# Third attention over the context: another order of four heads' work on every engine, turned groups in other banks

## The chip, the cores and the metric

The kernel runs on one core of one Trainium2 chip. The metric is the device time of one execution in microseconds. The kernel before took 2265.95 us (median of three runs, 2257.9 to 2266.71).

## The reference, cut to what matters

A perceiver of four layers works on 8 sequences of 64 rows with 256 features. In layers 0, 2 and 3 the rows attend to a context of 1601 rows with 128 features. The change touches the last of these, in layer 3, which computes for every batch and each of 16 heads of 16 features:

```
q = x @ Wq.T            k, v = ctx @ Wkv.T
p = softmax(q @ k.T * 16 ** -0.5)       # 64 x 1601 per head
o = (p @ v) @ Wo.T
```

The kernel keeps `p @ ctx` per head and multiplies with the value weights later, and it divides by the softmax's sums later too. Everything is float32: a product that needs the precision is made of three passes over a high and a low part (high x high, high x low, low x high).

## The kernel before, in words

The function `paired_attention` (L1126) holds the whole stage. A *unit* `v` is a pair of heads of one batch: 2 x 64 = 128 query rows, so there are 64 units, 8 per batch. Two units, that is four heads, are a *couple*: 32 couples, 4 per batch (`at` = 0 to 3). A *step* is two batches; the first step, the loop over the middle ones and the last are written by `loop_batches`. Per unit:

- TensorE makes the scores (L1285) in four products with 290, 512, 512 and 288 columns into PSUM banks 0 to 3. The first two are the first half, the last two the second.
- VectorE takes the maximum of each half (L1478, L1480) and joins the two (`ntop`, L1483).
- ScalarE takes the exponent of each half (`exponents`, L1420) into `normed` or `rooms`.
- TensorE turns the 13 chunks of 128 keys in four groups of 4, 4, 4 and 1 (`turn`, L1312) into banks 4, 5 and 7 (`turned_bank`, L1151).
- ScalarE copies each group rounded to `pTh` (`keep`, L1431), and VectorE subtracts it from the same bank into `pTl` (`low`, L1491). Only then is the bank free.
- Per couple TensorE multiplies the context's rows with both units' turned groups (`values`, L1344; its three passes are L616 to L618) in 39 products with 256 columns into bank 6, and VectorE stores the sum (`store`, L1501).

Beside this the keys of the *next* batch are projected, two tiles of 400 or 402 columns per couple (`key_tile`, L1291, three passes each), into bank 7. ScalarE copies a tile out (`keep_key`, L1410) into `key_rows`, POOL splits it (`split_key`, L1240 and L1243), and SyncE moves it in DMAs of 32 rows into `stacked`, the operand of the scores. Such a move (`move(b, at)`, L1184, with `move_half`, L2563) is 12 DMAs. For `at` = 0 and 2 it waits in SyncE's queue until the second scores of couples 1 and 3 are made, since those were the last to read what it overwrites; the move for `at` + 1 follows directly behind it. The other way round, `keep_key` for the first tile of a couple waits until the move that last read that half of `key_rows` has landed (semaphores `moved0`, `moved1`, L1405 to L1408). For couples 0 and 2 that is the move which the couple just before set off.

Every engine works through its own queue in the order written in its `body`. The order of TensorE for one couple before the change is: turn group 0 of the unit before, scores of unit `u`, turn 1, turn 2, values 0, turn 3, values 1, key tile 0, scores of `u + 1`, turn 0 and 1 of `u`, key tile 1, values 2, turn 2, values 3, turn 3. All semaphores count, so the number that an instruction waits for follows from the order.

Of the kernel before, what the change touches and what calls it, by code (L numbers as in the profile page):

```python
# [109 lines left out]
def perceiver_kernel(nc, dram, packs, out):  # L110
    with ExitStack() as stack:
# [1014 lines left out]
        def paired_attention(q, scale, keys, sums):  # L1126
# [8 lines left out]
            with ExitStack() as own, signals(nc, *names) as \  # L1135
# [15 lines left out]
                turned_bank = (4, 5, 7, 4), (5, 7, 4, 5)  # L1151
# [19 lines left out]
                with nc.Block() as block:  # L1171
# [98 lines left out]
                    def _(pe):  # L1270
                        def scores(u, step, first):
                            i = u // PER
                            v = step * UNITS + u
                            if first and i == 0:
                                pe.wait_ge(keys.first_moved[u], 48)
                            elif u % 4 == 0:
                                for sem in moved:
                                    pe.wait_ge(sem, MOVES * (2 * (2 * step + i) - 1 + (u % PER) // 4))
                            if u % 2 == 0:
                                pe.wait_ge(staged, step * COUPLES + u // 2 + 1)  # L1280
                            k, at = (u // 2) % 2, (u % 2) * P
                            for n in range(4):
                                if n in (0, 2) and not (first and u == 0):
                                    pe.wait_ge(probs_ready if n else probs_half, v)
                                last = pe.matmul(flat[:, score_cols[n]], qs[:, k, at:at + P],  # L1285
                                                 keys.stacked[:, u % PER, score_cols[n]], start=True, stop=True)
                                if n == 1:
                                    last.then_inc(scores_half, 1)
                            last.then_inc(scores_ready, 1)

                        def key_tile(u, step, j, final):  # L1291

                            i, at = u // PER, (u // 2) % 4
                            for chunk, tile, n in key_tiles(i, at, final):
                                if n == j:
                                    if at == 0 and j == 0:
                                        pe.wait_ge(low_ready, 2 * (2 * step + i) + 1)
                                    if j == 1:
                                        pe.wait_ge(key_kept, 8 * (2 * step + i) + 2 * at + 1)
                                    project_keys(pe, keys, chunk, tile, 7).then_inc(key_ready, 1)  # L1300

                        def key_bank_free(u, step, final):

                            i, at = u // PER, (u // 2) % 4
                            if key_tiles(i, at, final):
                                pe.wait_ge(key_kept, 8 * (2 * step + i) + 2 * at + 2)
# [9 lines left out]
                        def turn_first(g, v, early=False):  # L1316

                            if g == 0 and not early:
                                pe.wait_ge(low_kept, 4 * v - 1)
                            if g == 1 and not early:  # L1320
                                pe.wait_ge(low_kept, 4 * v)
                            if g == 3:
                                pe.wait_ge(low_kept, 4 * v + 1)
                            turn(g, v, 0)

                        def turn_second(g, v):

                            pe.wait_ge(low_kept, 4 * v + (-2, -1, 0, 1)[g])
                            turn(g, v, 1)

                        def values(g, c, i, early=False, new_batch=None):
# [7 lines left out]
                            pe.wait_ge(low_kept, 4 * (2 * c + 1) + g + 1)  # L1339
# [8 lines left out]
                        def body(step, first, final=False):  # L1348
                            for u in range(0, UNITS, 2):
# [6 lines left out]
                                if first and u == 0:  # L1356
                                    scores(u, step, first)
                                    scores(u + 1, step, first)
                                    for g in range(4):
                                        turn_first(g, v, True)  # L1360
                                    pe.wait_ge(low_kept, 3)
                                    key_tile(u, step, 0, final)
                                    key_tile(u, step, 1, final)
                                    continue
                                pe.wait_ge(probs_half, v)
                                turn_second(0, v - 1)
                                scores(u, step, first)
                                if first and u == 2:
                                    key_bank_free(0, step, final)
                                turn_second(1, v - 1)  # L1370
                                turn_second(2, v - 1)
                                values(0, c - 1, i, first and u == 2, new_batch)
                                turn_second(3, v - 1)
                                values(1, c - 1, i)
                                if key_tiles(u // PER, (u // 2) % 4, final):
                                    pe.wait_ge(low_kept, 4 * v - 2)
                                key_tile(u, step, 0, final)
                                scores(u + 1, step, first)
# [12 lines left out]
                        pe.wait_ge(probs_ready, last + 1)  # L1391
                        for g in range(4):
                            turn_second(g, last)
                        values(0, c, 1)
                        values(1, c, 1)
                        values(2, c, 1)
                        values(3, c, 1)

                    @block.scalar
                    def _(act):  # L1400
                        def keep_key(step, first_step, i, at, tile, j):
# [8 lines left out]
                            nc.scalar.activation(key_rows[:, cols], ps[:, 7, 0:cols.stop - cols.start], ACT.Copy)\  # L1410
# [14 lines left out]
                        def keep(g, v, slot, c=None):  # L1425

                            act.wait_ge(turned_ready, 4 * v + g + 1)
# [8 lines left out]
                        def body(step, first, final=False):  # L1436
                            for u in range(0, UNITS, 2):
# [32 lines left out]
                        for g in range(4):  # L1470
                            keep(g, last, 1)

                    @block.vector
                    def _(dve):
                        def maximum(v, slot):

                            dve.wait_ge(scores_half, v + 1)
                            dve.tensor_reduce(top[:, slot, 0:1], flat[:, half_cols[0]], AX.X, ALU.max).then_inc(top_step, 1)  # L1478
                            dve.wait_ge(scores_ready, v + 1)
# [6 lines left out]
                        def low(g, v, slot):  # L1486

                            dve.wait_ge(high_kept, 4 * v + g + 1)
# [37 lines left out]
                        for g in range(4):  # L1526
# [1806 lines left out]
```

## Time and profile before

| | us |
|---|---|
| median of three runs | 2265.95 |
| the profiled execution's own time | 2265.01 |
| its span, first to last instruction | 2263.2 |
| TensorE busy in the span | 2018.8 (89%) |
| VectorE busy | 1392.2 (62%) |
| ScalarE busy | 1141.2 (50%) |
| POOL busy | 595.6 (26%) |
| mean granted TensorE clock | 0.945 of full speed |

The stage that is changed runs from about 1700 to 2078 us of the span. In it the engines' rows show a pattern that repeats every couple, so one couple, read closely, tells most of the stage. Busy time of TensorE counts overlapping pieces: the distance between the starts of two matmuls, not the duration of one, tells what a matmul costs its queue.

### The profile page before, as it was taken

The page shows a single profiled execution, that of the slowest core. Times are in us where ns is not written, and L with a number is a line of the kernel's source. Part 1 is how long each engine was busy: PE and PEld are TensorE (multiplying, and loading weights), DVE is VectorE, ACT ScalarE, POOL GpSimd, SP SyncE. Part 2 cuts the span into 40 slices and gives each one's busy share as a digit, 9 for nine tenths or more (in the row PEclk, how much of TensorE's full clock was granted, in tenths as well). Part 3 has the DMA queues.
Part 4 walks back from the last instruction along what each step waited for, and adds up shares of the span by engine and source line. Part 5 has one row for each costly group of instructions (what it writes and reads, how often), then busy time and mean ns, then how long its engine had stood idle before and what let it go on. Part 6 is the DMA issues. An engine that isn't in the chain of part 4 may idle for free. (4 is left out here: it accounts for less than half of the span.)

```text
span 2263.2 us, 42827 instructions
## 1 busy us (share of the span) xinstructions
PE 2018.8 (89%) x14978; PEld 1739.0 (77%) x14978; DVE 1392.2 (62%) x2718; ACT 1141.2 (50%) x2324; POOL 595.6 (26%) x536
## 2 busy tenths in 40 slices
PE   5877999999887998589899999988888998998898
PEld 2766999999566885278699999966767888887677
DVE  8455777777355443831577777745456777776466
ACT  3235666666423432321566666633446676665254
POOL 2323212221012330200322222102325555440034
PEclk9798999999996998689999999999998999999899
DMA  5252101000041213431110110002226555551022
GB/s 217 58 233 103 42 31 46 30 30 0 36 149 58 79 54 138 191 133 64 59 46 31 36 39 30 0 0 84 80 71 164 152 138 139 139 132 42 19 79 76
DMA packets 49603, 183.66 MB, mean 81 GB/s; under 512 B 9392, under 2 KB 14896, under 8 KB 46128
## 3 DMA queue, kind: packets, MB, share of 16 engines
q1 hardware_dynamic: 49456, 181.75, 25.0%
q8 instruction: 86, 1.41, 0.3%
q14 instruction: 61, 0.50, 0.1%
HBM read 125.72 MB, written 13.90 MB: 62 GB/s over the span
## 5 line engine op out<-in xcount | busy, mean ns | idle before, releaser
L616 PE MATMUL ps<-pTh,ch 128*128 128x256 f32 (+1 forms) x1248 | 382.3, 306 | 26.2 <-DVE pTl L1491 25.0
L1026 ACT ACTIVATE pTh<-ps 128x512 fp32r<-128x512 f32 (+1 forms) x512 | 235.8, 519 | 258.0 <-PE ps L926 257.7
L617 PE MATMUL ps<-pTl,ch 128*128 128x256 f32 (+1 forms) x1248 | 350.2, 281 | 0.0
L618 PE MATMUL ps<-pTh,cl 128*128 128x256 f32 (+1 forms) x1248 | 349.9, 280 | 0.0
L1084 DVE TENSOR_TENSOR pTl<-ps,pTh 128x512 fp32r<-128x512 f32 (+1 forms) x512 | 277.3, 583 | 83.8 <-ACT pTh L1026 83.2
L616 PEld LDWEIGHTS ps<-pTh,ch 128*128 128x128 f32 (+1 forms) x1248 | 236.1, 189 | 43.0 <-DVE pTl L1491 32.4
L617 PEld LDWEIGHTS ps<-pTl,ch 128*128 128x128 f32 (+1 forms) x1248 | 236.9, 190 | 0.0
L618 PEld LDWEIGHTS ps<-pTh,cl 128*128 128x128 f32 (+1 forms) x1248 | 235.9, 189 | 0.0
L616 PE MATMUL ps<-cTh,qh 128*128 128x512 f32 (+2 forms) x512 | 184.8, 361 | 16.7 <-POOL ql L880 11.9
L618 PE MATMUL ps<-cTh,ql 128*128 128x512 f32 (+2 forms) x512 | 179.9, 351 | 0.0
L617 PE MATMUL ps<-cTl,qh 128*128 128x512 f32 (+2 forms) x512 | 179.5, 351 | 0.0
L1071 DVE TENSOR_REDUCE top<-ps 128x1 f32<-128x802 f32 x128 | 126.3, 987 | 75.2 <-PE ps L618 75.2
L1491 DVE TENSOR_TENSOR pTl<-ps,pTh 128x512 fp32r<-128x512 f32 (+1 forms) x256 | 138.8, 582 | 47.8 <-ACT pTh L1431 47.1
L1431 ACT ACTIVATE pTh<-ps 128x512 fp32r<-128x512 f32 (+1 forms) x256 | 117.7, 514 | 56.1 <-PE ps L1312 56.0
L1073 DVE TENSOR_REDUCE top<-ps 128x1 f32<-128x799 f32 x128 | 125.9, 983 | 10.4 <-PE ps L618 3.8
L1015 ACT ACTIVATE normed<-ps,ntop 128x802 f32<-128x802 f32 (+1 forms) x128 | 117.8, 926 | 20.4 <-DVE ntop L1076 19.1
L926 PE MATMUL ps<-ident,probs 128*128 128x128 f32 (+1 forms) x832 | 122.0, 273 | 2.8 <-ACT probs L1015 1.7
L926 PE MATMUL ps<-ident,normed 128*128 128x128 f32 (+1 forms) x832 | 123.5, 275 | 0.4 <-DVE pTl L1084 0.4
L616 PEld LDWEIGHTS ps<-cTh,qh 128*128 128x128 f32 x512 | 97.9, 191 | 30.6 <-POOL ql L880 13.6
L616 PE MATMUL ps<-xh,wgh 128*128 128x512 f32 (+1 forms) x280 | 113.3, 405 | 5.4 <-DVE gated L1942 4.3
L1015 ACT ACTIVATE probs<-ps,ntop 128x802 f32<-128x802 f32 (+1 forms) x128 | 117.9, 937 | 0.0
L617 PE MATMUL ps<-xl,wgh 128*128 128x512 f32 (+1 forms) x280 | 112.6, 402 | 0.0
(406 smaller groups left out, 4613.2 us busy)
## 6 DMA issues: line engine op xcount, KB each, us to landing
stacked<-weights SPq DMA_DIRECT2D x168, 100.2 KB, 2.2
stacked<-weights SPq DMA_DIRECT2D x168, 100.0 KB, 2.2
w<-l1f_w_in SPq DMA_DIRECT2D x16, 1024.0 KB, 8.2
wg<-l0f_guide_in SPq DMA_DIRECT2D x10, 704.0 KB, 5.2
z<-ctx_in SPq DMA_DIRECT2D x8, 832.0 KB, 12.8
z<-z SPq DMA_DIRECT2D x8, 832.0 KB, 10.0
keys<-ctx_in SPq DMA_DIRECT2D x8, 832.0 KB, 10.7
zT<-zT SPq DMA_DIRECT2D x8, 801.0 KB, 9.1
```

The costliest lines, as they stand in the source:

```text
L616: pe.matmul(out, high, moving_high, start=start, stop=False)
L617: pe.matmul(out, high, moving_low, start=False, stop=False)
L618: return pe.matmul(out, low, moving_high, start=False, stop=stop)
L926: last = pe.transpose(ps[0:w, turned_bank[slot][g], k * P:(k + 1) * P], probs[slot][:, chunk * P:chunk * P + w], ident[:])
L1015: nc.scalar.activation(probs[slot][:, cols], flat[:, cols], ACT.Exp, bias=ntop[:, slot:slot + 1], scale=scale, accum_out=sums[:, bass.ds(2 ...
L1026: nc.scalar.activation(pTh[0:w, PARTS[g][0]:PARTS[g][0] + n, slot, :], ps[0:w, turned_bank[slot][g], 0:n * P].rearrange("p (k r) -> p k r" ...
L1071: dve.tensor_reduce(top[:, slot, 0:1], flat[:, half_cols[0]], AX.X, ALU.max).then_inc(top_step, 1)
L1073: dve.tensor_reduce(top[:, slot, 1:2], flat[:, half_cols[1]], AX.X, ALU.max)\
L1084: dve.tensor_tensor(pTl[0:w, at, slot, :], ps[0:w, turned_bank[slot][g], 0:n * P].rearrange("p (k r) -> p k r", r=P), pTh[0:w, at, slot, : ...
L1431: nc.scalar.activation(pTh[0:w, PARTS[g][0]:PARTS[g][0] + n, slot, :], ps[0:w, turned_bank[slot][g], 0:n * P].rearrange("p (k r) -> p k r" ...
L1491: dve.tensor_tensor(pTl[0:w, at, slot, :], ps[0:w, turned_bank[slot][g], 0:n * P].rearrange("p (k r) -> p k r", r=P), pTh[0:w, at, slot, : ...
```

## The change: what it does

- The scores' halves become separate steps (`first_scores`, `second_scores`), and so do the maxima on VectorE.
- TensorE's order for a couple is now: first scores of `u`, turn group 0 of the unit before, key tile 0, key tile 1, second scores of `u`, turn 1, turn 3, turn 2, values 0, values 1, first and second scores of `u + 1`, turn 1, 0, 2 of `u`, values 2, values 3, turn 3.
- Groups of the even unit go to banks 7, 4, 5, 4, those of the odd unit to 7, 4, 7, 5; the key tiles go to banks 4 and 5 instead of 7.
- ScalarE's order: keep 0, both key tiles, keep 1, keep 3, first exponent, keep 2, second exponent, keep 1, keep 0, first exponent of `u + 1`, keep 2, keep 3, second exponent of `u + 1`.
- VectorE's order: first maximum, low 0, second maximum, low 1, 3, 2, both maxima of `u + 1`, low 1, low 0, store, low 3, low 2.
- The waits' numbers follow the new orders. POOL's and SyncE's programs, the number of instructions and their shapes stay as they are.

```diff
-                turned_bank = (4, 5, 7, 4), (5, 7, 4, 5)
+                turned_bank = (7, 4, 5, 4), (7, 4, 7, 5)
+                turn_place, low_place = ((2, 1, 3, 4), (1, 2, 4, 3)), ((2, 1, 4, 3), (1, 2, 4, 3))
+                key_bank = 4, 5
...
                         def key_tile(u, step, j, final):
...
-                                    if j == 1:
-                                        pe.wait_ge(key_kept, 8 * (2 * step + i) + 2 * at + 1)
-                                    project_keys(pe, keys, chunk, tile, 7).then_inc(key_ready, 1)
+                                project_keys(pe, keys, tiles[j][0], tiles[j][1], key_bank[j]).then_inc(key_ready, 1)
...
-                                pe.wait_ge(probs_half, v)
-                                turn_second(0, v - 1)
-                                scores(u, step, first)
-                                turn_second(1, v - 1)
-                                turn_second(2, v - 1)
-                                values(0, c - 1, i, first and u == 2, new_batch)
-                                turn_second(3, v - 1)
-                                values(1, c - 1, i)
-                                if key_tiles(u // PER, (u // 2) % 4, final):
-                                    pe.wait_ge(low_kept, 4 * v - 2)
-                                key_tile(u, step, 0, final)
-                                scores(u + 1, step, first)
-                                turn_first(0, v)
-                                turn_first(1, v)
-                                key_tile(u, step, 1, final)
-                                values(2, c - 1, i)
-                                key_bank_free(u, step, final)
-                                turn_first(2, v)
-                                values(3, c - 1, i)
-                                turn_first(3, v)
+                                first_scores(u, step, first)
+                                pe.wait_ge(low_kept, 4 * v - 6)
+                                turn(0, v - 1, 1)
+                                pe.wait_ge(low_kept, 4 * v - 5)
+                                key_tile(u, step, 0, final)
+                                pe.wait_ge(low_kept, 4 * v - 4)
+                                key_tile(u, step, 1, final)
+                                second_scores(u, step, first)
+                                key_bank_free(u, step, 0, final)
+                                turn(1, v - 1, 1)
+                                key_bank_free(u, step, 1, final)
+                                turn(3, v - 1, 1)
+                                pe.wait_ge(low_kept, 4 * v - 3)
+                                turn(2, v - 1, 1)
                                 values(0, c - 1, i, first and u == 2, new_batch)
                                 values(1, c - 1, i)
+                                first_scores(u + 1, step, first)
+                                second_scores(u + 1, step, first)
+                                turn(1, v, 0)
+                                pe.wait_ge(low_kept, 4 * v)
+                                turn(0, v, 0)
+                                turn(2, v, 0)
                                 values(2, c - 1, i)
                                 values(3, c - 1, i)
+                                pe.wait_ge(low_kept, 4 * v + 1)
+                                turn(3, v, 0)
...
                                 if before:
                                     keep(0, v - 1, 1)
+                                    for chunk, tile, j in tiles:
+                                        keep_key(step, first, i, at, tile, j)
                                     keep(1, v - 1, 1)
+                                    keep(3, v - 1, 1)
+                                exponents(v, 0, first and u < 2, 0)
+                                if before:
                                     keep(2, v - 1, 1)
-                                exponents(v, 0, first and u < 2, 0)
                                 exponents(v, 0, first and u < 2, 1)
-                                if before:
-                                    keep(3, v - 1, 1)
-                                    for chunk, tile, j in tiles[0:1]:
-                                        keep_key(step, first, i, at, tile, j)
+                                keep(1, v, 0, c if before else None)
                                 keep(0, v, 0, c if before else None)
-                                keep(1, v, 0, c if before else None)
-                                if before:
-                                    for chunk, tile, j in tiles[1:]:
-                                        keep_key(step, first, i, at, tile, j)
                                 exponents(v + 1, 1, first and u < 2, 0)
-                                exponents(v + 1, 1, first and u < 2, 1)
                                 keep(2, v, 0, c if before else None)
                                 keep(3, v, 0, c if before else None)
+                                exponents(v + 1, 1, first and u < 2, 1)
...
+                                first_maximum(v, 0)
                                 if before:
                                     low(0, v - 1, 1)
-                                maximum(v, 0)
+                                second_maximum(v, 0)
                                 if before:
                                     low(1, v - 1, 1)
+                                    low(3, v - 1, 1)
                                     low(2, v - 1, 1)
-                                    low(3, v - 1, 1)
-                                maximum(v + 1, 1)
+                                first_maximum(v + 1, 1)
+                                second_maximum(v + 1, 1)
+                                low(1, v, 0)
                                 low(0, v, 0)
-                                low(1, v, 0)
                                 if before:
                                     store(c - 1, 2 * step + (u - 2) // PER, ((u - 2) // 2) % 4)
+                                low(3, v, 0)
                                 low(2, v, 0)
-                                low(3, v, 0)
```

## Rows read from the trace of the kernel before

**Rows 1.** Busy time of each engine by stretch (stretch, its length, engines in turn).

```profile
core 0: us, PE busy (x) PEld busy (x) DVE busy (x) ACT busy (x) POOL busy (x), PEclk, DMA share, GB/s
1750.00:1800.00 50.00, 45.64 (x344) 42.55 (x343) 38.28 (x66) 34.88 (x77) 28.59 (x31) 1.00 0.58 146
...
1950.00:2000.00 50.00, 45.31 (x340) 42.22 (x339) 37.35 (x65) 34.64 (x78) 24.72 (x28) 1.00 0.55 141
```

**Rows 2.** Waits from 1720 to 2070 us: who for whom, total, times, longest.

```profile
ACT pTh L1431 <- PE ps L1312: 51.2, 61, 2.3
...
PEld ps L616 <- DVE pTl L1491: 32.4, 30, 2.2
PE ps L616 <- DVE pTl L1491: 25.0, 30, 2.0
```

**Rows 3.** Timeline, start of a couple at `at` = 2 (start, us, engine, line).

```profile
1867.14 0.27 PE L1312 MATMUL ps<-ident,rooms 128*65 128x128 f32 x1
...
1867.46 1.28 DVE L1491 TENSOR_TENSOR pTl<-ps,pTh 128x512 fp32r<-128x512 f32 x2
...
1868.20 0.38 PE L616 MATMUL ps<-pTh,ch 128*128 128x256 f32 x1 [0.80 <-DVE pTl L1491]
...
1868.54 0.28 PE L618 MATMUL ps<-pTh,cl 128*128 128x256 f32 x1
1868.66 0.28 PE L616 MATMUL ps<-pTh,ch 128*128 128x256 f32 x1
...
1870.11 0.34 PE L618 MATMUL ps<-cTh,wkl 128*128 128x402 f32 x1
1870.29 0.90 PE L1285 MATMUL ps<-stacked,qs 96*128 96x290 f32 x4
...
1870.58 0.51 ACT L1410 ACTIVATE weights<-ps 128x402 f32<-128x402 f32 x1 [0.81 <-PE ps L618]
...
1871.03 1.04 PE L1312 MATMUL ps<-ident,normed 128*128 128x128 f32 x8
```

**Rows 4.** Timeline of TensorE's weight loads at eight turns and what follows them.

```profile
1859.33 0.93 PEld L1312 LDWEIGHTS ps<-ident,normed 128*128 128x128 f32 x8
...
1860.22 0.19 PEld L616 LDWEIGHTS ps<-cTh,wkh 128*128 128x128 f32 x1
```

**Rows 5.** Timeline of VectorE, the last couples, which project no keys.

```profile
2040.50 0.98 DVE L1478 TENSOR_REDUCE top<-ps 128x1 f32<-128x802 f32 x1
...
2051.41 0.98 DVE L1478 TENSOR_REDUCE top<-ps 128x1 f32<-128x802 f32 x1
```

**Rows 6.** Timeline of SyncE's queue: starts of pairs of moves, 24 DMAs each.

```profile
1836.53 15.72 SPq L2569 DMA_DIRECT2D stacked<-weights  x24
...
1859.65 16.36 SPq L2569 DMA_DIRECT2D stacked<-weights  x24
...
1882.79 15.21 SPq L2569 DMA_DIRECT2D stacked<-weights  x24
```

**Rows 7.** Timeline: the scores ahead of that second start; ScalarE's first tile at `at` = 0.

```profile
1858.72 0.90 PE L1285 MATMUL ps<-stacked,qs 96*128 96x290 f32 x4
...
1859.46 1.04 PE L1312 MATMUL ps<-ident,normed 128*128 128x128 f32 x8
...
1847.45 0.51 ACT L1410 ACTIVATE weights<-ps 128x402 f32<-128x402 f32 x1 [0.80 <-PE ps L618]
```

**Rows 8.** Tile `stacked`, DMAs issued around 1844.0 us: the first move's last two.

```profile
L2569 SPq DMA_DIRECT2D stacked<-weights x2: 597/598/599, 1843.4 to 1844.0; - x2
...
DMA to landing us min/median/max: 2.2/2.2/2.2
```

**Rows 9.** Waits from 1583 to 1590 us, in the feed-forward stage.

```profile
PE ps L616 <- DVE gated L1942: 4.3, 1, 4.3
```

**Rows 10.** Busy time and granted clock behind two pauses of TensorE.

```profile
1889.00:1890.96 1.96, 0.00 (x0) 0.00 (x0) 0.74 (x2) 1.37 (x3) 1.96 (x1) 0.96 0.70 163
1890.96:1894.20 3.24, 3.24 (x15) 3.24 (x16) 3.15 (x5) 1.02 (x2) 1.33 (x3) 0.50 0.70 166
...
1589.08:1593.90 4.82, 4.79 (x11) 3.80 (x12) 2.48 (x4) 2.23 (x4) 2.37 (x1) 0.50 0.36 109
```

More of the change, by code:

```diff
@@ L1270, in _, with first_scores @@
                     def _(pe):
-                        def scores(u, step, first):
+                        def first_scores(u, step, first):
                             i = u // PER
@@ L1280, in scores, with second_scores @@
                                 pe.wait_ge(staged, step * COUPLES + u // 2 + 1)
+                            if not (first and u == 0):
+                                pe.wait_ge(probs_half, v)
+                            score_half(u, 0).then_inc(scores_half, 1)
+                        def second_scores(u, step, first):
+                            if not (first and u == 0):
+                                pe.wait_ge(probs_ready, step * UNITS + u)
+                            score_half(u, 1).then_inc(scores_ready, 1)
@@ L1281, in scores, with score_half @@
+                        def score_half(u, half):
                             k, at = (u // 2) % 2, (u % 2) * P
-                            for n in range(4):
-                                if n in (0, 2) and not (first and u == 0):
-                                    pe.wait_ge(probs_ready if n else probs_half, v)
+                            for n in (2 * half, 2 * half + 1):
                                 last = pe.matmul(flat[:, score_cols[n]], qs[:, k, at:at + P],
                                                  keys.stacked[:, u % PER, score_cols[n]], start=True, stop=True)
-                                if n == 1:
-                                    last.then_inc(scores_half, 1)
@@ L1289, in scores @@
-                            last.then_inc(scores_ready, 1)
+                            return last
                         def key_tile(u, step, j, final):
                             i, at = u // PER, (u // 2) % 4
[L1294 to L1297, printed above, removed]
-                                    if j == 1:
-                                        pe.wait_ge(key_kept, 8 * (2 * step + i) + 2 * at + 1)
-                                    project_keys(pe, keys, chunk, tile, 7).then_inc(key_ready, 1)
@@ L1302, in key_bank_free @@
-                        def key_bank_free(u, step, final):
+                            tiles = key_tiles(i, at, final)
+                            if tiles:
+                                if at == 0 and j == 0:
+                                    pe.wait_ge(low_ready, 2 * (2 * step + i) + 1)
+                                project_keys(pe, keys, tiles[j][0], tiles[j][1], key_bank[j]).then_inc(key_ready, 1)
+                        def key_bank_free(u, step, j, final):
                             i, at = u // PER, (u // 2) % 4
@@ L1305, in key_bank_free @@
                             if key_tiles(i, at, final):
-                                pe.wait_ge(key_kept, 8 * (2 * step + i) + 2 * at + 2)
+                                pe.wait_ge(key_kept, 8 * (2 * step + i) + 2 * at + j + 1)
                         def turn(g, v, slot):
@@ L1314, in turn @@
                             last.then_inc(turned_ready, 1)
[L1316 to L1329, printed above, removed]
                         def values(g, c, i, early=False, new_batch=None):
@@ L1338, in values @@
                                 pe.wait_ge(keys.first_rows, 1)
-                            pe.wait_ge(low_kept, 4 * (2 * c + 1) + g + 1)
+                            if g < 3:
+                                pe.wait_ge(low_kept, 4 * (2 * c + 1) + low_place[1][g])
                             for chunk in PARTS[g]:
@@ L1356, in body @@
                                 if first and u == 0:
-                                    scores(u, step, first)
-                                    scores(u + 1, step, first)
-                                    for g in range(4):
-                                        turn_first(g, v, True)
+                                    for n in range(2):
+                                        first_scores(u + n, step, first)
+                                        second_scores(u + n, step, first)
@@ L1361, in body @@
+                                    turn(1, v, 0)
+                                    turn(0, v, 0)
+                                    turn(2, v, 0)
+                                    pe.wait_ge(low_kept, 1)
+                                    turn(3, v, 0)
                                     pe.wait_ge(low_kept, 3)
                                     key_tile(u, step, 0, final)
+                                    pe.wait_ge(low_kept, 4)
                                     key_tile(u, step, 1, final)
@@ L1364, in body @@
                                     continue
-                                pe.wait_ge(probs_half, v)
-                                turn_second(0, v - 1)
-                                scores(u, step, first)
+                                first_scores(u, step, first)
+                                pe.wait_ge(low_kept, 4 * v - 6)
+                                turn(0, v - 1, 1)
                                 if first and u == 2:
-                                    key_bank_free(0, step, final)
@@ L1370, in body @@
-                                turn_second(1, v - 1)
-                                turn_second(2, v - 1)
+                                    pe.wait_ge(key_kept, 2)
+                                pe.wait_ge(low_kept, 4 * v - 5)
[4 more added lines that the diff above has]
+                                key_bank_free(u, step, 0, final)
@@ L1377, in body @@
-                                key_tile(u, step, 0, final)
-                                scores(u + 1, step, first)
-                                turn_first(0, v)
-                                turn_first(1, v)
-                                key_tile(u, step, 1, final)
+                                first_scores(u + 1, step, first)
+                                second_scores(u + 1, step, first)
+                                turn(1, v, 0)
+                                pe.wait_ge(low_kept, 4 * v)
@@ L1382, in body @@
+                                turn(0, v, 0)
+                                turn(2, v, 0)
                                 values(2, c - 1, i)
-                                key_bank_free(u, step, final)
-                                turn_first(2, v)
                                 values(3, c - 1, i)
-                                turn_first(3, v)
+                                pe.wait_ge(low_kept, 4 * v + 1)
+                                turn(3, v, 0)
                         loop_batches(pe, body)
@@ L1391, in _ @@
                         pe.wait_ge(probs_ready, last + 1)
-                        for g in range(4):
[L1393 to L1397, printed above, removed]
+                        pe.wait_ge(low_kept, 4 * last - 2)
+                        turn(0, last, 1)
+                        pe.wait_ge(low_kept, 4 * last)
+                        turn(1, last, 1)
+                        turn(3, last, 1)
+                        pe.wait_ge(low_kept, 4 * last + 1)
+                        turn(2, last, 1)
+                        for g in range(4):
+                            values(g, c, 1)
                     @block.scalar
@@ L1409, in keep_key @@
                             cols = K_COLS[tile]
-                            nc.scalar.activation(key_rows[:, cols], ps[:, 7, 0:cols.stop - cols.start], ACT.Copy)\
+                            nc.scalar.activation(key_rows[:, cols], ps[:, key_bank[j], 0:cols.stop - cols.start], ACT.Copy)\
                                 .then_inc(key_kept, 1)
@@ L1425, in keep @@
                         def keep(g, v, slot, c=None):
-                            act.wait_ge(turned_ready, 4 * v + g + 1)
+                            act.wait_ge(turned_ready, 4 * v + turn_place[slot][g])
                             if c is not None:
@@ L1469, in _ @@
                         last = STEPS * UNITS - 1
-                        for g in range(4):
+                        for g in (0, 1, 3, 2):
                             keep(g, last, 1)
@@ L1474, in _, with first_maximum, second_maximum @@
                     def _(dve):
-                        def maximum(v, slot):
+                        def first_maximum(v, slot):
                             dve.wait_ge(scores_half, v + 1)
                             dve.tensor_reduce(top[:, slot, 0:1], flat[:, half_cols[0]], AX.X, ALU.max).then_inc(top_step, 1)
+                        def second_maximum(v, slot):
                             dve.wait_ge(scores_ready, v + 1)
@@ L1486, in low @@
                         def low(g, v, slot):
-                            dve.wait_ge(high_kept, 4 * v + g + 1)
+                            dve.wait_ge(high_kept, 4 * v + turn_place[slot][g])
                             w, n = keys_in(PARTS[g][-1]), len(PARTS[g])
@@ L1508, in body @@
                                 before = not (first and u == 0)
+                                first_maximum(v, 0)
                                 if before:
                                     low(0, v - 1, 1)
-                                maximum(v, 0)
+                                second_maximum(v, 0)
                                 if before:
                                     low(1, v - 1, 1)
+                                    low(3, v - 1, 1)
                                     low(2, v - 1, 1)
-                                    low(3, v - 1, 1)
-                                maximum(v + 1, 1)
+                                first_maximum(v + 1, 1)
+                                second_maximum(v + 1, 1)
+                                low(1, v, 0)
                                 low(0, v, 0)
-                                low(1, v, 0)
                                 if before:
                                     store(c - 1, 2 * step + (u - 2) // PER, ((u - 2) // 2) % 4)
+                                low(3, v, 0)
                                 low(2, v, 0)
-                                low(3, v, 0)
                         loop_steps(dve, body)
                         last = STEPS * UNITS - 1
-                        for g in range(4):
+                        for g in (0, 1, 3, 2):
                             low(g, last, 1)
```

## The prediction

> **What bounds the kernel now.** The change touches one stage, 1700 to 2078 us, so I read the busy times of that stretch first: TensorE is busy 45.6 of 50 us, VectorE 38, ScalarE 35, and the clock is full [rows 1]. TensorE is the bound, but not quite. The waits say what it lacks: in 30 of the 32 couples its value products wait for `low` on VectorE, 25.0 us in all [rows 2]. The timeline shows the place. TensorE ends turn group 3 at about 1867.3 and starts values 1 only at 1868.20, since `low(1)` stands on VectorE behind both maxima and `ntop`, starts at 1867.46 and takes 0.6 to 0.7 us [rows 3]. So each couple has a hole of 0.8 to 0.9 us, and a second one near 0.5 us at turn 1.
>
> How long is a couple? Pairs of moves start at 1836.53, 1859.65 and 1882.79, one pair per two couples [rows 6]: two couples take 23.1 us. And what is TensorE's own work in a couple? From starts to starts a value product costs 0.12 us (1868.54 to 1868.66), the scores of a unit 0.74 (1870.29 to 1871.03), a key product 0.18 to 0.19 [rows 3], and eight turns 0.89, or 0.112 each [rows 4]. With 39 products, 26 turns, two sets of scores and six key products: 4.68 + 2.91 + 1.49 + 1.11 = 10.2 us. Two couples are 20.4, so about 2.7 us per two couples is waiting. That is all that a better order can win here.
>
> **The change, part by part.**
>
> *The holes.* On VectorE `low 0` now stands between the two maxima, and turns, values and key tiles are spread so that `low(1)` is asked for only after the 12 products of values 0. I laid the four queues out side by side with the durations above, the ScalarE and VectorE operations at their distances in the same rows (a `keep` and a `low` 0.5 and 0.6 us, a maximum 0.9 to 1.0, an exponent 0.9), and went through several couples until they repeated. Leaving the DMAs out, TensorE hardly waits any more: 10.3 us per couple. The old order laid out alike gives 11.5 against the measured 11.56, and 10.9 for the last couples without key tiles, as measured (2040.50 to 2051.41 [rows 5]). So, by itself, the new order would give back 1.2 us per couple, some 30 us in all. VectorE is busy 38.3 of 50 us and ScalarE 34.9 [rows 1], that is 8.9 and 8.1 us per couple, so neither becomes the bound.
>
> *The key tiles against the moves.* This decides. In couples 0 and 2 of a batch, ScalarE's first key copy waits until the move that the previous couple set off has landed. Take T, the start of that move: it is set off when the second scores of `u + 1` are made, 0.19 us after TensorE goes on (1859.46 to 1859.65) [rows 6, 7]. A pair of moves issues 24 DMAs in 15.2 us, 0.634 apart (1882.79 row); the 12th is issued at T + 7.0, and a DMA lands 2.2 us after its issue [rows 6, 8]. The move is complete at T + 9.2. (In the pair of 1836.53 the 12th was issued at 1844.0 and landed at 1846.2, T + 9.7, since one issue was late.)
>
> Before the change ScalarE copied at 1847.45, T + 10.9, and even then it had waited for TensorE, not for the move [rows 7]. The slack was 1.2 to 1.7 us. Now both ends close in. The move's start is as late as before in the couple or later, and the copy stands right behind `keep 0` at the couple's head. From the end of the second scores TensorE has only 12 turns (1.34), 15 value products (1.80), a turn (0.11), half the scores (0.37), four turns (0.45) and key tile 0 (0.56): 4.63 us, and ScalarE can start 0.29 us after a key tile's last product (1870.29 to 1870.58) [rows 3]. That is T + 4.7. The move lands at T + 9.2. **ScalarE stops for 4.5 us.**
>
> Behind the stopped copy on ScalarE stand keep 1, keep 3 and the exponents of unit `u`. On TensorE the second key tile and the second scores (0.93 us) can still run, to T + 5.4; then turn 1 waits for the key copy, because it shares bank 4 with key tile 0 now. VectorE has its second maximum and then waits for keep 1. Nothing useful is left: TensorE stands from T + 5.4 to T + 9.8 (9.2, a wake-up of 0.05 and 0.54 for the copy), 4.4 us.
>
> From there to the next T, two couples' work less what was done ahead: 20.4 - 4.63 - 0.93 = 14.8 us, then 0.19, then next T. The cycle is 9.8 + 14.8 + 0.2 = 24.8, and with two short waits of about 0.1 us each that my layout shows in front of key tiles and turns, 25.0 us. Before it was 23.1. The 1.9 us more come although all the old holes are gone.
>
> How often: the wait is there in couple 2 of batches 0 to 6 and couple 0 of batches 1 to 6 (the last batch projects nothing): 13 times. 13 x 1.9 = +25 us.
>
> The move for odd `at` has its last issue at T + 14.6, is complete at T + 16.8, and is wanted a whole couple after the first, at T + 19.6: covered. The same for the scores' own waits for `stacked`, three couples on. POOL's splits and SyncE's context fetches gain time.
>
> *The clock.* A pause of 4.4 us in TensorE has a second price. In this stage a pause of 1.96 us (1889.00 to 1890.96, at the loop's turn) was followed by 3.24 us at half clock, in which 15 value products ran [rows 10]: 0.216 us each instead of 0.12, 1.44 us lost. A pause of 4.3 us near 1585, the nearest in length to mine, was followed by 4.82 us at half clock [rows 9, 10]; at the same ratio 2.1 us lost. The regular pauses of 0.8 us cost no clock (1.00 in rows 1). After the new stall TensorE runs without a pause to the next T, so nothing hides the loss. I take 2.0 us, with 0 and 2.8 as ends: 13 x 2.0 = +26 us.
>
> *The rest.* Six couples' worth lie outside these cycles (two first, four last). They save 0.6 to 1.2 us each: -4 us. The pause at the loop's turn (1.96 us [rows 10]) falls partly under a stall: -1 us. New banks and counts cost nothing by themselves: same bytes, same shapes, and the bank shared by key tile 0 and turn 1 is priced above. Extra `wait_ge` on TensorE: 0 to 0.05 us, hidden by queued products; up to +3 us.
>
> *Sum:* 25 + 26 - 4 - 1 = **+46 us**, on the profiled execution's 2265.0: **2311 us**. That execution is 1 us under the median of the runs, which changes nothing.
>
> One rule of the Trainium skill speaks to the move's length. The row gives 12 DMAs of 100 KB in 9.2 us. "DMA: Bandwidth & Descriptors", section "Bandwidth", gives 435 GB/s for transfers inside SBUF; by that, an estimate from the page, 1.2 MB would pass in 2.8 us and land near T + 5, and the stall would all but vanish. Here SyncE's issues, 0.63 us apart, set the pace, so the measurement decides and the rule gives only a small chance to the second rival.
>
> **Rivals.**
>
> 1. *Stall without a clock loss.* The half-clock stretch lies in the pause, or the turns and products behind it need little. Then only the 1.9 us remain: 25 - 5 = +20, **2285 us**. For it: low stretches start at varying points of a pause. Against: both pauses above were followed by full stretches. Chance 0.17.
> 2. *The moves are no obstacle, so the change is faster.* Place: `keep_key` at couples 0 and 2. It decides the sign at a landing of about T + 7.3 instead of T + 9.2 (a cycle of 23.1 us) without the clock's price, and below T + 4.7 nothing waits. Then all holes go: about -30 us, **2236 us**. For it: everything else in the layout favours the change. Against: 14 pairs of moves show the 0.63 us spacing. Chance 0.12.
> 3. *The two cancel*, the stall shorter by some 2 us and only part of the clock lost: **2266 us**. Chance 0.04.
> 4. *Dearer.* Moves complete at T + 10.4 where an issue is late, or half clock lasts 6 us: +12 to +20 more, **2327 us**. Chance 0.06.
>
> My forecast has the remaining 0.61. The range 2282 to 2330 takes in rivals 1 and 4. A change under 0.5% (11 us) can't be told from none here. Faster 0.12, same 0.04, slower 0.84.
>
> **What would show it.** In the waits after, ScalarE's L1410 would wait for DMA `stacked`, 13 times, near 4.5 us each; L1312 on TensorE would wait for ScalarE L1410 for about 4.4. Starts of pairs of moves would lie 26 to 28 us apart, the two couples between them about 16.5 and 10.3. The 25 us of L616 waiting for `low` would be gone. The granted clock would fall about 13 times, by 0.5 for 3 to 5 us each. The stage would end 46 us later. I am wrong if L1410 still waits for TensorE alone: then the couples shrink to 10.3 us and rival 2 holds. If the starts lie 25.0 apart and the clock stays at 1.00, it is rival 1.

## The result

The changed kernel takes 2312.07 us (median of four runs, 2310.33 to 2315.02), the kernel before 2261.93 us in the same series. The ratio is 1.0224, with a 95% interval of 1.0192 to 1.0255: 2.2% slower. The profiled execution took 2315.02 us, against 2265.01 before: +50.0 us. I had forecast +46 and, from the profiled execution of before, 2311 us. So the step was 4 us larger than forecast. That the median lies only 1 us from 2311 is partly luck, since this series' median of before is 3 us below the 2265.0 from which I added up.

The difference lies in the stage that was changed. The first halves' maxima span it in both traces. Of the kernel before:

```profile
L1478 DVE TENSOR_REDUCE top<-ps x64: 979/993/994, 1699.6 to 2067.2; 128x1 f32<-128x802 f32 x64
```

and of the changed kernel (the line is now L1481):

```profile
L1481 DVE TENSOR_REDUCE top<-ps x64: 979/992/996, 1702.5 to 2118.1; 128x1 f32<-128x802 f32 x64
```

That is 367.6 us and 415.6 us: +48.0. The stage also began 2.9 us later, and 0.9 us came back behind it.

The waits of the changed kernel from 1720 to 2120 us (who for whom, total, times, longest) show what took the place of [rows 2]:

```profile
DVE pTl L1497 <- ACT pTh L1437: 83.4, 45, 5.6
...
ACT weights L1416 <- DMA stacked<-weights: 55.4, 13, 5.4
PE ps L1318 <- ACT weights L1416: 54.8, 13, 5.2
...
PEld ps L616 <- DVE pTl L1497: 1.8, 11, 0.2
```

TensorE's value products (L616) no longer wait for `low`: 25.0 us before, and now only their weight loads show a row, of 1.8 us. In its place stand 13 waits of ScalarE for a move, 4.3 us each, and 13 of TensorE for ScalarE's key copy, 4.2 us each. In the stretches of [rows 1] TensorE's busy time falls in the first, and its clock in both:

```profile
1750.00:1800.00 50.00, 39.87 (x274) 37.32 (x273) 30.93 (x54) 29.23 (x65) 19.64 (x24) 0.86 0.53 133
1950.00:2000.00 50.00, 45.94 (x313) 43.21 (x314) 32.66 (x57) 32.28 (x72) 24.57 (x28) 0.88 0.46 117
```

The second stretch shows why busy time misleads: TensorE is busy 45.9 of 50 us as before, but with 313 matmuls instead of 340, since at half clock each takes longer.

One stall, read in the timeline of the changed kernel (start, us, engine, line):

```profile
1886.06 13.92 SPq L2577 DMA_DIRECT2D stacked<-weights  x22
...
1890.65 0.40 PE L616 MATMUL ps<-cTh,wkh 128*128 128x400 f32 x1
...
1891.26 0.54 PE L1295 MATMUL ps<-stacked,qs 96*128 96x512 f32 x2
...
1895.18 0.90 ACT L1416 ACTIVATE weights<-ps 128x402 f32<-128x402 f32 x2 [4.16 <-DMA stacked<-weights]
1895.74 1.78 PEld L1318 LDWEIGHTS ps<-ident,rooms 128*128 128x128 f32 x9 [4.29 <-ACT weights L1416]
1895.74 2.18 PE L1318 MATMUL ps<-ident,rooms 128*128 128x128 f32 x9 [3.94 <-ACT weights L1416]
```

The move starts at T = 1886.06. Both key tiles and the second scores are done at 1891.8, T + 5.7. The copy starts at T + 9.1, and TensorE goes on at T + 9.7. The granted clock in the pause, behind it and later:

```profile
1891.80:1895.70 3.90, 0.00 (x0) 0.00 (x0) 1.36 (x3) 0.52 (x2) 0.00 (x0) 0.75 0.69 161
1895.74:1900.60 4.86, 4.86 (x23) 4.86 (x24) 1.57 (x3) 3.39 (x8) 2.77 (x4) 0.50 0.66 159
1900.60:1905.00 4.40, 4.40 (x38) 4.31 (x38) 2.55 (x4) 1.39 (x3) 1.12 (x2) 1.00 0.86 243
```

The mean granted clock of 0.75 in the pause says that it fell there, and it stays at 1.2 GHz for 4.86 us behind it. The 23 matmuls there, 9 turns and 14 products, would take 9 x 0.112 + 14 x 0.12 = 2.7 us at full clock, so 2.2 us are lost.

SyncE's queue gives the cycle of two couples, against [rows 6]:

```profile
1749.08 16.38 SPq L2577 DMA_DIRECT2D stacked<-weights  x24
...
1886.06 15.19 SPq L2577 DMA_DIRECT2D stacked<-weights  x24
...
1913.19 15.17 SPq L2577 DMA_DIRECT2D stacked<-weights  x24
...
2022.28 16.20 SPq L2577 DMA_DIRECT2D stacked<-weights  x24
```

From 1749.08 to 2022.28 are ten cycles of 27.3 us; before, one took 23.1. All twelve from the first pair to the thirteenth (1721.85 to 2049.51) took 327.7 us, against 279.4 before (1721.59 to 2000.95): +48.3 us, which is the whole growth of the stage.

### The profile page after: what moved, and what is told of

Same layout as the page of the kernel before. It is cut to its first block and busy times, and to the rows that moved or that the text cites. A ratio compares the mean times of both kernels' runs of the same rounds, so it can differ in the third digit from the quotient of the medians.

```text
span 2313.2 us, 42768 instructions
## 1 busy us (share of the span) xinstructions
PE 2042.1 (88%) x14978; PEld 1762.3 (76%) x14978; DVE 1392.1 (60%) x2718; ACT 1144.4 (49%) x2324; POOL 594.7 (26%) x536
## 5 line engine op out<-in xcount | busy, mean ns | idle before, releaser
L616 PE MATMUL ps<-pTh,ch 128*128 128x256 f32 (+1 forms) x1248 | 386.9, 310 | 1.2 <-DVE pTl L1084 1.2
L617 PE MATMUL ps<-pTl,ch 128*128 128x256 f32 (+1 forms) x1248 | 357.3, 286 | 0.0
L618 PE MATMUL ps<-pTh,cl 128*128 128x256 f32 (+1 forms) x1248 | 356.3, 286 | 0.0
L616 PEld LDWEIGHTS ps<-pTh,ch 128*128 128x128 f32 (+1 forms) x1248 | 245.0, 196 | 10.5 <-DVE pTl L1084 8.2
L617 PEld LDWEIGHTS ps<-pTl,ch 128*128 128x128 f32 (+1 forms) x1248 | 245.0, 196 | 0.0
L618 PEld LDWEIGHTS ps<-pTh,cl 128*128 128x128 f32 (+1 forms) x1248 | 243.6, 195 | 0.0
L616 PE MATMUL ps<-cTh,qh 128*128 128x512 f32 (+2 forms) x512 | 184.8, 361 | 15.6 <-POOL ql L880 10.8
L1073 DVE TENSOR_REDUCE top<-ps 128x1 f32<-128x799 f32 x128 | 125.9, 983 | 10.4 <-PE ps L618 3.8
L1318 PE MATMUL ps<-ident,rooms 128*128 128x128 f32 (+1 forms) x416 | 69.9, 315 | 58.1 <-ACT weights L1416 54.8
L616 PEld LDWEIGHTS ps<-cTh,qh 128*128 128x128 f32 x512 | 97.8, 191 | 29.8 <-POOL ql L880 12.8
L616 PE MATMUL ps<-xh,wgh 128*128 128x512 f32 (+1 forms) x280 | 113.3, 405 | 5.6 <-DVE gated L1950 4.3
```

Of the source, the lines that this page charges most:

```text
L616: pe.matmul(out, high, moving_high, start=start, stop=False)
L617: pe.matmul(out, high, moving_low, start=False, stop=False)
L618: return pe.matmul(out, low, moving_high, start=False, stop=stop)
L1073: dve.tensor_reduce(top[:, slot, 1:2], flat[:, half_cols[1]], AX.X, ALU.max)\
L1318: last = pe.transpose(ps[0:w, turned_bank[slot][g], k * P:(k + 1) * P], probs[slot][:, chunk * P:chunk * P + w], ident[:])
```

## The experiments

**Early moves (e1).** The changed kernel; only SyncE's queue differs. The three DMAs of a unit's keys wait for that unit's scores, not all twelve for the last ones.

```diff
-                            if at % 2 == 0:
-                                sp.wait_ge(scores_ready, 8 * b + 4 + 2 * at)
-                            move_half(sp, keys, key_highs, key_lows, at // 2, at % 2, moved[at % 2])
+                            for j in range(4):
+                                if at % 2 == 0:
+                                    sp.wait_ge(scores_ready, 8 * b + 2 * at + j + 1)
+                                move_head(sp, keys, key_highs, key_lows, at // 2, at % 2, moved[at % 2], j)
```

> The changed kernel, with SyncE's queue alone altered: the 12 DMAs of a move no longer wait together for the couple's last scores; the three DMAs of each unit wait for that unit's scores. Nine of twelve are issued before T. My theory (ScalarE's key copy waits for the move): the last three land near T + 3.5, the copy is wanted at T + 4.7, so L1416's waits for DMA fall from 55 us to under 3, TensorE's 4 us pauses and the half-clock stretches go, two couples take 20.7 to 21 us instead of 27.3, and the kernel takes about 2236 us, 25 us less than the kernel before. Rival (the pauses come from TensorE's own order and the shared bank 4, and the DMA is only the last of several waits): the pauses shrink by 1 to 2 us at most and the time stays above 2280.

Measured: 2231.77 us, 0.9874 of the kernel before (0.9841 to 0.9907), so 1.3% faster than it and 80 us faster than the changed kernel. Starts of couples on VectorE in its timeline:

```profile
1779.63 0.98 DVE L1482 TENSOR_REDUCE top<-ps 128x1 f32<-128x802 f32 x1
...
1790.10 0.98 DVE L1482 TENSOR_REDUCE top<-ps 128x1 f32<-128x802 f32 x1
...
1800.50 0.98 DVE L1482 TENSOR_REDUCE top<-ps 128x1 f32<-128x802 f32 x1
```

A couple takes 10.4 us. From 1720 us on, no engine's wait for `stacked` is left in the list, and the busy times show TensorE without a hole:

```profile
1780.00:1840.00 60.00, 59.91 (x458) 56.24 (x457) 49.48 (x86) 46.95 (x103) 34.88 (x40) 1.00 0.64 159
```

One stall for a move is left, at the head of the stage. The first move began only at 1704.57, directly behind the copies of the first keys in SyncE's queue:

```profile
1716.48 0.90 ACT L1417 ACTIVATE weights<-ps 128x402 f32<-128x402 f32 x2 [4.33 <-DMA stacked<-weights]
1717.04 1.91 PE L1319 MATMUL ps<-ident,rooms 128*128 128x128 f32 x9 [4.12 <-ACT weights L1417]
```

The rival is out: bank 4 is still shared, the orders are the changed kernel's, and only the moves' start differs. This kernel beats both.

**The same queue of SyncE on the kernel before (e4).**

> The kernel before, with the same altered queue of SyncE as the first run. Theory: its key copies never waited for a move, so nothing changes: 2262 us, within 0.3%. Rival (early moves help by themselves, for example through less traffic at a bad moment): faster by 5 us or more.

Measured: 2265.74 us, ratio 1.0017 (0.9999 to 1.0035): no difference. So the 80 us between e1 and the changed kernel are not a merit of early moves as such, which give the old order nothing. They are what late moves cost the new order.

**A filled pause (e2).** The changed kernel with matmuls in TensorE's pause; nobody reads their results.

```diff
                                 second_scores(u, step, first)
+                                if u % 4 == 0 and key_tiles(u // PER, (u // 2) % 4, final):
+                                    pe.wait_ge(value_kept, c - 1)
+                                    for n in range(30):
+                                        pe.matmul(ps[:, 6, 2 * P:4 * P], keys.wkh[:, 0:P], keys.wkh[:], start=True, stop=True)
                                 key_bank_free(u, step, 0, final)
```

> The changed kernel, with 30 extra products of 256 columns (results unused, in the free half of bank 6) on TensorE right behind the second scores in couples 0 and 2 of batches 0 to 6, where it pauses. They fill about 3.6 us of the 3.9 us pause and add no work behind it. Theory (half of the loss is the clock): the clock stays at full speed, the DMA waits stay near 4 us each, two couples take about 25.0 to 25.3 us, and the kernel gets faster than the changed one by 20 to 26 us, to about 2288. Rival (the clock costs little, since the chain behind is set by ScalarE and VectorE): the time stays within 5 us of 2312.

Measured: 2292.48 us, ratio 1.0117 to the kernel before (1.0071 to 1.0163), some 20 us less than the changed kernel, though TensorE does more. The waits for the DMA are all still there, and over two cycles (1930.2 to 1980.35, so 25.1 us each) the clock is full:

```profile
ACT weights L1420 <- DMA stacked<-weights: 59.6, 13, 5.8
```

```profile
1930.20:1980.35 50.15, 49.33 (x378) 46.43 (x377) 34.83 (x61) 32.79 (x72) 24.62 (x29) 1.00 0.52 132
```

So there the stall alone makes a cycle of 25.1 us, and the clock adds 2.2 to make it 27.3. Earlier cycles of this run are longer, and one of the twelve (1722.37 to 2030.28, 307.9 us in all) still has a stretch at half clock behind a pause of 2.0 us:

```profile
1722.37:1748.79 26.42, 24.48 (x190) 23.26 (x189) 17.48 (x31) 16.48 (x36) 14.84 (x17) 1.00 0.53 141
...
1774.54:1802.58 28.04, 26.00 (x190) 24.76 (x189) 17.50 (x31) 16.49 (x36) 12.39 (x15) 0.94 0.47 118
```

The other eleven, all at full clock, take 24.9 to 26.4 us, 25.4 on average, and by them the clock's price is 1.9 us per cycle. Over the whole kernel it is 20 us, at the lower edge of what I expected; the stage itself is 23 us shorter in the profiled executions (392.5 against 415.6).

**Eight DMAs instead of twelve (e3).** The changed kernel without the second copy of the keys' high part, so one of the three passes of the scores meets stale keys.

```diff
-        MOVES = 16 * 12
+        MOVES = 16 * 8
...
-                for n, src in enumerate((high, high, low)):
+                for n, src in ((0, high), (2, low)):
```

> The changed kernel without the second copy of the keys' high part in a move: 8 DMAs instead of 12 (the scores' low query part then meets stale keys). The last DMA is issued at T + 4.4 and lands at T + 6.6. Theory: ScalarE waits 1.7 to 2.0 us instead of 4.3, TensorE pauses 1.4 to 1.7 us; without a clock loss two couples take about 22.5 us, with one of 1.4 us about 24; so the kernel takes 2257 to 2275 us. Rival (the wait is set by something else than the count of DMAs): the waits stay at 4 us each and the time near 2312.

Measured: 2254.47 us, ratio 0.9965 (0.9945 to 0.9984), 3 us below the expected range. The waits:

```profile
ACT weights L1416 <- DMA stacked<-weights: 20.8, 11, 2.6
PE ps L1318 <- ACT weights L1416: 20.3, 12, 2.4
```

They are 1.9 us each for ScalarE and 1.7 for TensorE, as expected: a third less of DMAs takes 2.4 us off each wait. What I got wrong is the clock, for most cycles. Four of them, from one start of moves to the fifth, and one pause inside:

```profile
1893.81:1983.71 89.90, 84.12 (x634) 78.27 (x633) 69.56 (x121) 65.52 (x144) 49.13 (x57) 1.00 0.43 111
1899.56:1900.90 1.34, 0.00 (x0) 0.00 (x0) 1.30 (x3) 0.54 (x2) 0.00 (x0) 1.00 0.69 160
```

89.9 / 4 = 22.5 us per cycle, exactly the sum without a clock loss. Nine of the twelve cycles are like this, at 22.3 to 22.9 us. Three took 24.4 to 24.9 us, with a mean clock of 0.93; here are two of them, and one at full clock between them:

```profile
1729.60:1754.50 24.90, 22.51 (x160) 21.21 (x159) 17.50 (x31) 16.47 (x36) 12.22 (x15) 0.93 0.38 101
...
1824.13:1846.99 22.86, 20.98 (x160) 19.56 (x159) 17.14 (x31) 16.47 (x36) 12.23 (x15) 1.00 0.43 111
...
1869.39:1893.81 24.42, 22.48 (x160) 21.10 (x159) 17.37 (x31) 16.53 (x36) 12.21 (x15) 0.93 0.38 103
```

TensorE's pause for the key copy in these three:

```profile
1737.71 1.97 PE L1318 MATMUL ps<-ident,rooms 128*128 128x128 f32 x9 [2.39 <-ACT weights L1416]
...
1831.74 1.20 PE L1318 MATMUL ps<-ident,rooms 128*128 128x128 f32 x9 [1.86 <-ACT weights L1416]
...
1877.05 1.40 PE L1318 MATMUL ps<-ident,rooms 128*128 128x128 f32 x9 [1.88 <-ACT weights L1416]
```

The eight pauses of 1.4 to 1.5 us in the twelve cycles left the clock alone, and those of 2.3 and 2.4 us did not. Of two of 1.9 us one did and one did not, so near that length more than the length decides, and no run here shows what. The profiled execution was also the quickest of ten (2244.46 us); how many low stretches the others had isn't known.

**Late moves on the kernel before (e6).** Its four engines' order is untouched.

```diff
-                                sp.wait_ge(scores_ready, 8 * b + 4 + 2 * at)
+                                sp.wait_ge(scores_half, 8 * b + 5 + 2 * at)
```

> The kernel before, with its four engines' order untouched, but the move set off later: it waits for the first half of the scores of the next couple instead of the last scores of its own, about 4.5 us later. Theory (what costs is the distance between a move's start and the copy, not the new order): the move then lands at about 13.7 us on the old scale where the copy is wanted at 10.9, so ScalarE waits 2.3 to 2.9 us for DMA 13 times, two couples take 25.3 us or a little more with a lower clock, and the kernel takes 2290 to 2308 us. Rival (the old order has room for a late move): within 5 us of 2262.

Measured: 2303.02 us, ratio 1.0187 (1.0155 to 1.0218).

```profile
ACT weights L1410 <- DMA stacked<-weights: 48.1, 13, 5.0
...
PE ps L616 <- ACT weights L1410: 25.6, 12, 3.2
```

The time is in the expected range. The waits are longer than I said, 3.7 us each, but the same picture arises from the old order: 13 waits for the DMA and 40 us more. What costs is the distance from a move's start to the copy, whichever end is shifted.

**One part of the new order undone (e5).** Early moves as in e1, with `low 0` ahead of both maxima again.

```diff
-                                first_maximum(v, 0)
                                 if before:
                                     low(0, v - 1, 1)
+                                first_maximum(v, 0)
                                 second_maximum(v, 0)
```

> The first run's kernel (new order, early moves), with one part of the new order undone: on VectorE, low 0 of the unit before stands again ahead of both maxima instead of between them. Theory (the gain of the new order is that TensorE no longer waits for VectorE, and the place of low 0 is part of it): VectorE's chain to the exponents gets longer by up to 0.6 us, TensorE gets a hole of 0.5 to 0.6 us per couple, a couple takes 10.9 us instead of 10.4, and the kernel 2245 us. Rival (the place of low 0 does not matter, only TensorE's own order does): 2232 us, a couple 10.4 us.

Measured: 2250.9 us, ratio 0.9948 (0.993 to 0.9967), 19 us more than e1. Two maxima one couple apart, and the wait that came back:

```profile
1792.20 0.98 DVE L1482 TENSOR_REDUCE top<-ps 128x1 f32<-128x802 f32 x1
...
1803.20 0.98 DVE L1482 TENSOR_REDUCE top<-ps 128x1 f32<-128x802 f32 x1
```

```profile
PEld ps L616 <- DVE pTl L1498: 17.8, 50, 0.8
```

A couple takes 11.0 us instead of 10.4. The whole stage, from its first maximum to its last, in e1 and here:

```profile
L1482 DVE TENSOR_REDUCE top<-ps x64: 979/992/994, 1689.4 to 2028.3; 128x1 f32<-128x802 f32 x64
```

```profile
L1482 DVE TENSOR_REDUCE top<-ps x64: 982/993/994, 1689.7 to 2041.2; 128x1 f32<-128x802 f32 x64
```

That is 338.9 and 351.5 us, 12.6 apart, close to the 13 that I had put. The medians are 19 apart, but the runs of e5 spread from 2238.6 to 2257.34, and the profiled one is the quickest of them. So 13 to 19 of the 31 us by which e1 beats the kernel before hang on where `low 0` stands on VectorE. The other parts of the order were not tried one by one.

## Why the prediction was right, step by step

- **The holes go.** Right: L616's 25.0 us of waiting vanished, and a couple without a DMA wait takes 10.4 us (10.3 forecast). e1 shows the gain nearly by itself, with one stall left: 30.8 us less than the kernel before, 28.7 of them in the stage of the profiled executions (338.9 against 367.6); 30 forecast.
- **The copy comes before the move has landed.** Right in place and count: 13 times. Copy at T + 9.1 (9.2), TensorE stops at T + 5.7 (5.4) and goes on at T + 9.7 (9.8). ScalarE's mean wait is 4.3 us (4.5). e1 and e6 move one end of that distance in either kernel and turn the stall off and on.
- **The cycle without the clock.** 25.0 forecast, 25.1 in e2's stretch of two, 25.4 on average of its eleven at full clock.
- **The clock's price.** 2.0 us per stall forecast. 2.2 are lost in the stretch shown, and e2 gives 27.3 - 25.1 = 2.2, or 1.9 by the average of eleven. The nearest row by length of pause (2.1 us [rows 10]) was the better guide than the one from the same stage (1.44).
- **The sum.** 13 x (27.3 - 23.1) = 54.6 us against 51 forecast, and the stage grew by 48.0, so the rest of the stage gave back 6.6 us against 5. So the stalls came out 4 us dearer and the rest 2 us cheaper, which partly cancelled; another 2 us arose outside the stage, where I had put none. Within the rest, the loop's turn was under-sized. Before, the cycle that holds it was 2.6 us longer than the others:

```profile
1882.79 15.21 SPq L2569 DMA_DIRECT2D stacked<-weights  x24
1908.53 15.21 SPq L2569 DMA_DIRECT2D stacked<-weights  x24
```

Now the eighth cycle, which holds it, takes 27.2 us (1913.19 to 1940.41), no longer than the rest: about 2.6 us came back there, and I had put 1. How the 54.6 us split between stall and clock is known to some 4 us only: 26 and 29 by e2's stretch of two, 30 and 25 by its eleven cycles; 25 and 26 forecast.

- **Rivals.** Stall without clock loss: out in this kernel, and it is what e2 approaches (2292 us; 2285 forecast). Moves no obstacle: out here, and what e1 makes true (2232 us; 2236 forecast). Its reason fell too: the key copy came at T + 9.1, not near T + 5 as by the estimate beside the forecast. What sets the spacing of 0.63 us, SyncE's issuing, as I wrote, or the transfer itself, no run here separates. The trace leans to the issuing: the 16 DMAs issued from 1886.1 to 1895.5 each landed 2.1 to 2.2 us after their issue, so none was held up behind an earlier one. The two cancel: out. Dearer: moves that issued late did occur, and TensorE's pauses there reached 5.2 us, but the mean stayed at 4.2.

## What to carry to other kernels

When an instruction moves up in its queue, measure the distance to everything it waits for, the DMAs first: 1.2 us of slack in the trace of before was the whole warning, and the copy moved up by 6 us. A transfer that waits for the last reader of a whole block can often start piece by piece behind each reader, which here turned a loss of 50 us into a gain of 31. And here a TensorE pause of some 4 us cost about 2 us more through the clock.

## What the runs showed of the hardware

The price of a pause is not proportional to it. The pauses of 1.4 to 1.5 us kept the clock at 1.00 (e3), of two of 1.9 us one was followed by a stretch at half clock and one was not (e3), and one of 3.9 us was followed by 4.86 us at half clock (the changed kernel). Filling a pause with 30 products whose results nobody reads made the kernel 20 us faster (e2), though it moved no transfer and ended no wait earlier.
